# A two-layer transformer kernel: mixture-of-experts tiles moved among the first layer's attention units

## The reference

```python
xn = layernorm(x)
x = x + attention(xn) + moe(xn)            # layer 0
xn = layernorm(x)
x = x + attn1(xn) + lowrank_ffn(xn)        # layer 1

def attention(x):                          # 16 heads of 16
    q, k, v = heads(x @ W_qkv + b_qkv)
    return softmax(q @ k.T) @ v            # no scale, no mask

def moe(x):                                # 4096 tokens, 8 experts
    aff = x @ centroids.T
    e = argmax(aff); alpha = sigmoid(aff[e])
    h = relu((layernorm(x) * g[e] + b[e]) @ w1[e].T + b1[e])   # 256 -> 1024
    y = x + h @ w2[e].T + b2[e]                                # 1024 -> 256
    return alpha * y + (1 - alpha) * x
```

## Time and profile before

| | us |
|---|---|
| runs of the kernel, median | 2216.59 |
| lowest, highest | 2209.68, 2216.69 |
| the profiled execution | 2201.47 |
| its span in the trace | 2199.7 |
| first exp of layer 0 starts | 79.8 |
| last product of layer 0's attention ends | 678.2 |
| experts on PE | 680.2 to 1012.1 |
| first matmul of the FFN | 1035.3 |
| PE busy, granted clock over the span | 85%, 0.936 |

### The profile page before, as it was taken

One profiled execution on the slowest core, in us unless ns is written; L12 is line 12 of the kernel. 1 busy time (PEld: TensorE's weight loads), 2 busy tenths in 40 slices (PEclk: granted clock), 3 DMA queues, 4 the chain that ended last, 5 costly groups with the idle time before them and its releaser, 6 DMA issues.

```text
span 2199.7 us, 31394 instructions
## 1 busy us (share of the span) xinstructions
PE 1877.1 (85%) x10777; PEld 880.9 (40%) x10777; DVE 1346.1 (61%) x4181; ACT 895.0 (41%) x1633; POOL 402.9 (18%) x651
## 2 busy tenths in 40 slices
PE   3788988888878999994688779989898989899877
PEld 2222332322214666663234334444444444444334
DVE  4888778777862333334553766667575757676553
ACT  0354555554552111111343344445354545444444
POOL 3332332223151111102442100000010101000000
PEclk8799988988998999997899899999999999999999
DMA  4445444432413111103104244253554534443440
GB/s 107 101 111 117 108 91 103 89 62 55 88 40 140 32 34 32 32 27 98 29 20 86 53 74 81 56 98 65 83 89 73 92 55 91 81 82 63 66 74 21
DMA packets 131219, 159.50 MB, mean 73 GB/s; under 512 B 22419, under 2 KB 115731, under 8 KB 129014
## 3 DMA queue, kind: packets, MB, share of 16 engines
q1 hardware_dynamic: 126630, 148.18, 34.0%
q0 software_dynamic: 4432, 9.33, 1.5%
HBM read 111.26 MB, written 46.19 MB: 72 GB/s over the span
## 4 chain that ended last, share of the span: by engine, by line
PE 55%; DVE 18%; DMA 10%; issue 5%; ACT 5%; POOL 4%; SPq 3%; DVEq 0%; POOLq 0%
PE p_PV L669 9%; PE p_S L631 6%; PE p_PV L749 6%; PE p_S L652 6%; DVE p_S L1006 5%; PE p_S L725 5%; PE p_Ma L845 5%; DVE t_mx L1012 4%; PE p_Ma L603 4%; SPq L1719 3%; DMA t_R<-ks 3%; ACT t_spl L1383 2%; DVE t_rr L966 2%; PE p_S L738 2%; DMA msd<-t_msp 2%
## 5 line engine op out<-in xcount | busy, mean ns | idle before, releaser
L1405 ACT ACTIVATE t_R<-p_S 128x512 f32<-128x512 f32 (+1 forms) x1216 | 660.3, 574 | 579.9 <-PE p_S L656 312.9
L1006 DVE CUSTOM_DVE_ANT_0 p_S<-p_S,t_maskq 128x128 f32<-128x128 f32 (+3 forms) x1024 | 472.9, 521 | 151.2 <-PE p_S L631 148.3
L631 PE MATMUL p_S<-t_R 96*128 96x512 bf16 (+3 forms) x1536 | 461.9, 347 | 107.6 <-DMA t_R<-ks 60.8
L652 PE MATMUL p_S<-t_R 99*128 99x512 bf16 (+3 forms) x1536 | 482.4, 339 | 28.9 <-ACT t_R L1405 11.5
L1012 DVE TENSOR_REDUCE t_mx<-p_S 128x1 f32<-128x512 f32 x512 | 330.0, 680 | 63.3 <-PE p_S L631 61.6
L669 PE MATMUL p_PV<-t_R 128*17 128x512 f32 (+3 forms) x3072 | 337.0, 512 | 8.9 <-ACT t_R L1405 8.7
L631 PEld LDWEIGHTS p_S<-t_R 96*128 96x128 bf16 x1536 | 136.3, 100 | 443.9 <-issue 155.5
L652 PEld LDWEIGHTS p_S<-t_R 99*128 99x128 bf16 x1536 | 152.0, 99 | 193.8 <-ACT t_R L1405 111.3
L1609 POOL CAST t_spl<-t_rr 128x512 bf16<-128x512 f32 x80 | 48.9, 611 | 970.6 <-DVE t_rr L966 970.6
L656 PE MATMUL p_S<-t_maskk,t_identb 128*128 128x128 bf16 x1024 | 195.5, 219 | 0.0
L1239 DVE TENSOR_SCALAR t_spl<-p_S,t_B1T 128x128 f32<-128x128 f32 x312 | 84.4, 342 | 135.8 <-PE p_S L738 135.7
(11 more groups left out here) (202 smaller groups left out, 1906.9 us busy)
## 6 DMA issues: line engine op xcount, KB each, us to landing
t_R<-qs SPq DMA_DIRECT2D x288, 128.0 KB, 4.2
t_R<-ks SPq DMA_DIRECT2D x288, 128.0 KB, 5.0
qs<-t_spl SPq DMA_DIRECT2D x48, 384.0 KB, 2.3
t_R<-in_w SPq DMA_DIRECT2D x16, 1024.0 KB, 6.2
ks<-t_spl SPq DMA_DIRECT2D x32, 384.0 KB, 5.3
ysd<-t_cT SPq DMA_DIRECT2D x39, 128.0 KB, 1.7
t_X<-in_x SPq DMA_DIRECT2D x8, 512.0 KB, 4.2
h0d<-t_cT SPq DMA_DIRECT2D x8, 512.0 KB, 2.9
```

Source lines behind the costliest of these rows:

```text
L631: t = self.nc.tensor.matmul(bank[:, z, :], qa[0:96, h, qb * 128:(qb + 1) * 128], ka[0:96, h, 0:n], start=True, stop=True)
L652: t = self.nc.tensor.matmul(bank[:, z, :], ka[0:99, h, kb * 128:(kb + 1) * 128], qa[0:99, h, n0:512], start=True, stop=not u.causal)
L1006: x = nc.vector.tensor_tensor_reduce(out=sc, in0=sc, in1=m.maskq[:, 512 - n:512], scale=1.0, scalar=NEG, op0=ALU.add, op1=ALU.max, accum_o ...
L1405: nc.scalar.activation(m.P1X[kb][j0 // per] if u.causal else m.P[p % 2][:, j0:j0 + per, :], m.s2_bank(k)[:, 0:per * n].rearrange("p (j n) ...
```

## The change

The steps of the experts are no longer a stage of their own but a lane in the rounds of units 2 to 13, and what they need is made beforehand.

- **Order.** `weave` takes the place of `interleave` in layer 0: each lane's steps are counted in a dry walk first, and spread evenly over the round ((k + 0.5) / n).
- **Norms first.** `norms(0)` (batch 0), `norms(1)` (batches 1 and 2) and `norms(2)` (batches 3 to 7) all stand ahead of the first exp: statistics, xn, transposes, affinity, h0. h0 (the norm of the norm) is one activation of X on ScalarE (`twice`, L1543), with a scale from two Newton iterations on GpSimd, four operations a batch into one buffer; the store of the batch before must have landed. xT, one buffer, is stored to DRAM (`xTd`) for batches 1 to 7 and read back when a batch's projection comes (`load_x`, 512 KB).
- **Round of unit 0**: ScalarE turns X into X + xn (L1552, 32 operations; before, GpSimd) and issues the 16 loads of half the weights (L1569, L1571, 0.5 MB each). **Unit 1**: `route`, then `scatter` (L1852).
- **Two passes.** R1 holds the weights of half of the 1024 inner features of all experts. Pass 0 runs in the rounds of units 2 to 7, 40 steps a round (a tile has 6), with gather, head, up, turn, down; it stores the tile's transposed input to `hTd` and its half result with bias to `ysd`. Weights of the other half are loaded in unit 8's round, and pass 1 runs in those of units 9 to 13 (a tile has 5 steps): SP reads `hTd` back, and the half result is added to `ysd` by an accumulating DMA on GpSimd (L1876). The number of the expert is loaded into a register by PE in both passes, and by ScalarE in both (78 times each).
- **Engines and banks.** The relu (four a half tile, L1649) is ScalarE's, not VectorE's. Max scores have two S1 banks in layer 0; the third joins Ma and Mb in one rotation for projections and experts. The product that was drained at the end of each unit now comes in the next round (only the last unit drains it).
- The FFN's first steps wait for the last result, the causal masks of layer 1 are made later on GpSimd, and some tiles of the FFN lie elsewhere.

```diff
 def layer0(e):
-    first = e.norm0(UNITS0[0])
...
-        lanes = [(first, 6) if i == -2 else (lane(e.norm0, i + 3), 1)]
-        e.loads0(i)
...
-        if i == 13:
-            lanes.append((e.route(), 1))
-        if i == 14:
-            lanes.append((e.scatter(), 1))
...
-    pipeline(UNITS0, -2, e.expp, e.maxp, e.pre0, extra)
+    u = UNITS0
+    weave(e, e.norms(0))
+    weave(e, chain(e.pre0(u[0], 1), e.pre0(u[1], 20)), e.norms(1), e.bias2())
+    e.attention_init()
+    weave(e, e.maxp(u[0]), e.norms(2))
+    first, second = e.experts(0), e.experts(1)
+    for i in range(16):
+        lanes = [e.expp(u[i])]
+        if i < 15:
+            lanes.append(e.maxp(u[i + 1]))
+        if i < 14:
+            lanes.append(e.pre0(u[i + 2]))
+        if i == 0:
+            lanes += [e.base(), e.weights(0)]
+        if i == 1:
+            lanes.append(chain(e.route(), e.scatter()))
+        if 2 <= i < 8:
+            lanes.append(take(first, 40 if i < 7 else 60))
+        if i == 8:
+            lanes.append(e.weights(1))
+        if 9 <= i < 14:
+            lanes.append(take(second, 40 if i < 13 else 60))
+        weave(e, *lanes)
...
 class VectorE(Engine):
-    def turn(self, t):
...
 class ScalarE(Engine):
+    def twice(self, b, k):
+        e.wait_ge(s.rstd0, 2 * GROUP[b] + 2)
+        if b:
+            e.wait_ge(s.d_h0, 16 * b)
+        x = self.nc.scalar.activation(m.h0b[:, k, :], m.X[:, t, :], ACT.Identity, bias=m.bsa[:, t:t + 1],
+                                      scale=m.rsa[:, t:t + 1])
...
+        for k in range(4):
+            x = self.nc.scalar.activation(
+                m.AT[:, k, :], m.MB[i][:, k * 128:(k + 1) * 128], ACT.Relu,
+                bias=m.B1T[:, bass.ds(self.regs[t], 1), 4 * p + k:4 * p + k + 1])
...
 class SyncE(Engine):
+    def fetch(self, p, t):
+        if p == 0:
+            return
+        e.wait_ge(s.d_hts[t % 2], 16 * (t // 2 + 1))
+        e.wait_ge(s.up_mm, TM + max(t - 1, 0))
+        self.start(m.hT[t % 2], m.hTd[t], s.d_ht[t % 2])
```

More of the change, by code:

```diff
@@ L481, in layer1_init, with causal_masks, bank, norms @@
     def layer1_init(self): pass
-    def norm0(self, u):
-        return none() if u.c else steps(24)
-    def pre0(self, u):
-        return steps(3 if u.c else 6)
-    def maxp(self, u):
-        return steps(s1_uses(u))
+    def causal_masks(self): pass
+    def bank(self):
+        self.banks += 1
+        return self.banks % 3
+    def norms(self, i):
+        for b in GROUPS[i]:
+            for k in range(4):
+                self.stats(b, k)
+                yield
+        self.seed0(i, 0)
+        yield
+        self.newton0(i, 0)
+        yield
+        for b in GROUPS[i]:
+            for k in range(4):
+                self.normal(b, k)
+                yield
+            for c in range(2):
+                self.turn_x(b, c, self.bank())
+                yield
+            self.affinity(b, self.bank())
+            yield
+        self.seed0(i, 1)
+        yield
+        self.newton0(i, 1)
+        yield
+        for b in GROUPS[i]:
+            for k in range(4):
+                self.twice(b, k)
+                yield
+    def stats(self, b, k): pass
+    def seed0(self, i, j): pass
+    def newton0(self, i, j): pass
+    def normal(self, b, k): pass
+    def turn_x(self, b, c, i): pass
+    def affinity(self, b, i): pass
+    def twice(self, b, k): pass
+    def base(self):
+        for b in range(NB):
+            for k in range(4):
+                self.add_norm(b, k)
+                yield
+    def add_norm(self, b, k): pass
+    def pre0(self, u, idle=9):
+        if u.c == 0 and u.b:
+            self.load_x(u.b)
+            yield
+        for z in range(2):
+            self.project0(u, z, self.bank())
+            yield
+        self.project0(u, 2, self.bank())
+        yield from steps(idle)
+    def load_x(self, b): pass
+    def project0(self, u, z, i): pass
+    def weights(self, p):
+        for x in range(NE):
+            for z in range(2):
+                self.load_w(p, x, z)
+                yield
+    def load_w(self, p, x, z): pass
     def bias2(self):
@@ L495, in route, with routing @@
     def route(self):
+        self.route_bank = self.bank()
+        yield from self.routing()
+    def routing(self):
         return steps(46)
@@ L499, in scatter, with experts, lead, rise @@
         return steps(32)
+    def experts(self, p):
+        self.experts_begin(p)
+        self.fetch(p, 0)
+        self.fetch(p, 1)
+        yield
+        yield from self.lead(p, 0)
+        yield from self.rise(p, 0)
+        yield from self.lead(p, 1)
+        if p == 0:
+            self.fetch(p, 2)
+        for t in range(TM):
+            ahead = t + 3 - p
+            if ahead < TM:
+                self.fetch(p, ahead)
+            self.turn(p, t, self.bank())
+            yield
+            if t + 1 < TM:
+                yield from self.rise(p, t + 1)
+            if t + 2 < TM:
+                yield from self.lead(p, t + 2)
+            i = self.bank()
+            for h in range(2):
+                self.down(p, t, h, i)
+                yield
+    def lead(self, p, t):
+        if p == 0:
+            self.head(t, self.bank())
+            yield
+    def rise(self, p, t):
+        i = self.bank()
+        for c in range(2):
+            self.up(p, t, c, i)
+            yield
+    def experts_begin(self, p): pass
+    def fetch(self, p, t): pass
+    def head(self, t, i): pass
+    def up(self, p, t, c, i): pass
+    def turn(self, p, t, i): pass
+    def down(self, p, t, h, i): pass
+    def maxp(self, u):
+        return steps(s1_uses(u))
     def gathers(self, b):
@@ L742, in down @@
[L742 to L757 removed]
+        n = p * TM + t
@@ new lines, in turn, with down @@
+    def turn(self, p, t, i):
+        e, m, s, n = self.e, self.m, self.s, p * TM + t
+        e.wait_ge(s.turn_mm, n + 1)
+        if n:
+            e.wait_ge(s.y_mm, n)
+        for k in range(4):
+            x = self.nc.scalar.activation(
+                m.AT[:, k, :], m.MB[i][:, k * 128:(k + 1) * 128], ACT.Relu,
+                bias=m.B1T[:, bass.ds(self.regs[t], 1), 4 * p + k:4 * p + k + 1])
+        x.then_inc(s.turn_done, 1)
+    def down(self, p, t, h, i):
+        e, m, s, n = self.e, self.m, self.s, p * TM + t
+        if h == 0:
+            return
+        e.wait_ge(s.y_mm, n + 1)
+        if n >= 2:
+            sems, before = (s.d_y, n - 2) if n - 2 < TM else (s.d_ya, n - 2 - TM)
+            e.wait_ge(sems[before % 2], 16 * (before // 2 + 1))
+        self.nc.scalar.copy(m.Y[n % 2], m.MB[i][:, 0:256]).then_inc(s.y_done, 1)
```

926 lines of the change are left out of this document (487 added, 439 removed).

## The result

The changed kernel takes 2289.73 us on the median of four runs (2281.48 to 2294.83), the kernel before 2216.64 (2209.68 to 2223.61): ratio 1.0326, 95% interval 1.0279 to 1.0373. It is slower by 73 us. The profiled executions stand 80.0 apart, 2279.7 against 2199.7. The forecast, 2252, had the sign and a little under half of the size (+35 for +73); the range, 2195 to 2308, holds the time. The profiled execution of the changed kernel lies 8 us under its median and that of the kernel before 15 under its own, so the profiles stand further apart than the medians.

What follows compares the result with a forecast made beforehand. PE stood empty 7.6 to 10.4 us of each attention unit, holes expert tiles could fill. Terms 150 + 40 + 48 + 30 + 683 + 42 + 55 = 1048 against 1012 before: +36, forecast 2252 us, range 2195 to 2308.

Steps and rivals of the forecast that it cites:

- Term 1: Start of layer 0: all norms and h0 stand ahead of the first exp, which comes at 150 instead of 79.8.
- What bounds, and what the change pays per tile: Attention units leave PE empty 7.6 to 10.4 us each; a halved tile costs 4.36 plus 3.94, together 8.3 as before.
- Term 2: Rounds of units 0 and 1: 88 us, 40 for ScalarE's work in unit 0 and 48 for unit 1 with routing.
- Term 3: Scatter: PE's first head in unit 2 waits for the gather, a hole of 27, plus 3 for slow PE: 30 us.
- Term 4: Eleven host units, 2 to 7 and 9 to 13: 628 of slots plus register loads, fetches and reloads, 683 us.
- rival A: Host units: PE runs in slots alone, 636 instead of 683, kernel 2206; sign: host waits below about 44; chance 0.17.
- Term 5: Rest of layer 0: unit 8 with the weights' reload 42 us, units 14 and 15 together 55.
- B: Start is shorter: batches' chains overlap and the scatter's hole is filled, 40 us less, 2213; chance 0.07.
- C: Host units: holes don't fill, attention and expert streams only add, 736 us, kernel 2305; chance 0.18.

Runs made afterwards that it cites:

- e3_warm: Changed kernel with extra matmuls keeping PE busy in the norms of batches 3 to 7; first exp 171.6 (was 174.4), unit 15 closes at 1095.3 (was 1094.6).
- e2_weights_early: Changed kernel with the first half weights loaded during unit 0's max scores and norms; unit 0's round 46.8 us (was 52.2), unit 15 closes 5 us earlier, at 1089.2.
- e5_cover: Changed kernel with pass 0 in the rounds of units 3 to 7 instead of 2 to 7; unit 2's round 68.5 us, unit 15 closes at 1103.3, 9 later.
- e8_cover_gidx: Kernel of e5_cover with the gidx load issued by GpSimd, not SP; round 2 43.6 us (was 68.5), round 1 78.3 (was 51.4), unit 15 closes at 1099.9.
- e1_behind: Changed kernel with both expert passes after the last attention unit; span 2405.9 us against 2279.7.
- e9_no_w1load: Changed kernel with the second half weights' loads cut to a sixteenth of the bytes (wrong weights); unit 8's round 54.0 us against 55.9.
- e6_spread: Changed kernel reordered: norms of batches 2 to 7 in unit 0's round, gidx and pass 1's reads on GpSimd; that round 147 us, unit 15 closes at 1056.4.
- e4_h0_late: Changed kernel with h0 of batches 3 to 7 moved into unit 0's round; first exp 157.6 (was 174.4), unit 0 closes at 236.2, ten us later.

## Why the prediction missed the size

Layer 0 with the experts was to end 36 us later than before and ended 82.5 later. The mechanism of the sum was right where it says that PE's holes fill. What failed is the size of the parts in which PE's holes don't fill: above all term 1, the serial start (150, measured 174.4), then unit 8 (42, measured 55.9), unit 0 (40, measured 52.2) and unit 1 with the scatter's hole. The waits and the slow clock behind them follow, term by term.

| term | forecast | measured |
|---|---|---|
| first exp | 150 | 174.4 |
| unit 0 | 40 | 52.2 |
| unit 1 and the scatter's hole | 78 | 85.1 |
| units 2 to 7 and 9 to 13 | 683 | 342.8 + 327.6 = 670.4 |
| unit 8 | 42 | 55.9 |
| units 14 and 15 | 55 | 56.6 |
| sum | 1048 | 1094.6 |

- **What bounds, and what the change pays per tile**: right for pass 0. Its six rounds should have 336 us of slots, 55.9 each, and took 342.8, 57.1 each: halving the tiles cost PE nothing that shows. Pass 1 should have 292 and took 327.6; with its reads in the other queue 302.1.
- **Term 1** named the path rightly and under-sized its links. The xT store of batch 1 was issued at 58.7, not 52.5, batch 2's affinity ended at 69.2, not 59, and the memsets were done at 83, not 72:

```profile
58.67 7.21 SPq L1960 DMA_DIRECT2D xTd<-t_xTb  x2
```

  These 10 us stayed. Then the five batches, from the first normalisation (103.9) to the first of the last h0 operations (152.2), took 48 us and not 34: a batch took 8.5 to 9.4, not 6. Of these 14 us e3_warm shows 12 to be the half clock. I had put the half clock in the upper end of the range (160). It belonged in the sum: PE was busy 37.0 of 48 us there, in turns with waits for the other engines, and the granted clock was 0.50 from 104 to 152. The h0 chain, 22 us, was right.
- **Term 2**: unit 0 was mis-sized by 12. I summed ScalarE's work, 39; but the round first waits 3.0 for xT's reload, projects at half clock (3.78 for the four records that take 1.88 later), and its late transfers compete with the weights (5 us, e2_weights_early).
- **Term 3**: the size was near (a wait of 29.4 for 27; 85.1 for 78 in all), and the scatters began 34 us into the round (260.9), not 28. The cause was incomplete. I said that PE's head alone stood behind the scatters. SP's queue stood there too, so a cover for the head alone gains nothing (e5_cover). What a cover for both is worth stays open: e8_cover_gidx lost to the 18.9 us on VectorE what it had gained in unit 2's round. I had written that an error in unit 1 cancels against this term, and did not look at gidx in SP's queue.
- **Term 4**: 670 for 683, but by two errors that offset each other. Pass 0's rounds came at 57.1, rival A's 57; pass 1's, of units 9 to 12, took 62 and 72 to 73 in turn, 67.6 on the mean, where I gave 60 to 66. SP's place for the reads cost 18.8 of PE's waits (forecast 23), and moving them gave 25. Register loads cost no wait that the trace shows: PE's queue takes 0.30 us for one at the median (39 in pass 0; 0.30 in the kernel before as well), while PE works off what is queued. That is half of the floor that the Trainium skill gives (page "DMA: Bandwidth & Descriptors", section "Latency and other measured facts"); for these loads the trace decides.
- **Term 5**: unit 8 was under-sized by 14, since I took a bare unit of the changed kernel to be one of before. It is not: in e1_behind an even one takes 43 to 46, of which the third bank explains 2.4 and the wait for xT's reload 2.7. In e9_no_w1load, 4.65 more are the wait for pass 1's first read.
- **Rivals.** A had host rounds in slots alone, 636 in all. Its sign, waits under 44 us in the host rounds, came true by a hair (670 less 628 of slots is 42), so the number alone doesn't part it from the forecast; by place it held in pass 0 and not in pass 1. The kernel is slower all the same, as the four other terms were too small, each on the side of waiting. B's condition was false, and e6_spread and e4_h0_late show that the start isn't hidden by moving it into one round. C is refuted by pass 0, where PE was busy 338.0 of 342.8 us, and by e1_behind, where the same work in separate stages costs 126 more.

## What to carry to other kernels

Filling the holes of one stage with the work of another paid as the slots said, to within 2% a round in pass 0; what decided was what had to be made ready beforehand. All of it ahead of the first exp put that 95 us later; six batches in one round made that round 147 us long; two batches in each of three rounds gave rounds of 54, 46 and 50, and the only version faster than the kernel before. The versions differ in other things as well, so read it as a good first try and not as a law: cut a serial chain over engines into pieces that each fit in the slack of one round, with other steps between the links. When work is moved next to a slow step, list each queue that waits for that step in order (here PE's head and SP's gidx) before counting on a cover for one of them.
